# Five pairs of two experts run ahead of the last scatters, in a routed feed-forward kernel on one core

## The reference, cut to what matters

```python
xn = layernorm(x)                                  # 8192 tokens of 256
s = recurrent_attention(xn, W_in, W_g, W_out)      # a gated scan with 8 states, and projections
w, idx = gate(xn, wg)                              # 4 of 32 experts for every token
fe = idx.reshape(-1)
pos = (jnp.cumsum(one_hot(fe), axis=0) * one_hot(fe)).sum(-1) - 1
keep = pos < cap                                   # cap = 1280 rows for each expert, in token order
xe = xp[buf_tok].reshape(E, cap, DIM)
h = silu(xe @ w1) * (xe @ w3)                      # per expert, 256 x 256 weights
out = (h @ w2) * buf_w
y = zeros.at[buf_tok].add(out)
z = silu(xn @ sw1) * (xn @ sw3) @ sw2              # the shared expert
return x + s * silu(y + z)
```

## Time and profile before

| | |
|---|---|
| median of 3 runs | 1230.02 us (1228.3 to 1236.38) |
| the profiled execution | 1240.9 us, span 1239.0 us |
| phase A ends on TensorE | 482.2 us |
| the first expert matmul | 506.37 us |
| TensorE busy in the span | 82% |
| VectorE, POOL busy in the span | 66%, 61% |

### The profile page before, as it was taken

The page is one execution under the profiler, slowest core; times in us unless marked ns, Lnnn a source line. Parts: engine busy times, 40 slices in busy tenths (PEclk is TensorE's granted clock), DMA queues, the critical chain, the costliest instruction groups (busy, mean ns, idle before and its releaser), DMA issues.

```text
span 1239.0 us, 29972 instructions
## 1 busy us (share of the span) xinstructions
PE 1010.5 (82%) x7997; PEld 982.2 (79%) x7997; DVE 814.1 (66%) x2699; ACT 604.1 (49%) x1315; POOL 750.0 (61%) x600
## 2 busy tenths in 40 slices
PE   6767767778775763699999999999999999999900
PEld 5667666667664653699999999999999999999900
DVE  5656655555454454477777777777777777777659
ACT  5657656555664662244444444444444444445323
POOL 1255655566454656266776766667576767667785
PEclk7987988787887886799999999999999999999955
DMA  9123332223222334588787878878888889888579
GB/s 315 49 94 113 109 109 94 102 105 109 90 98 84 109 112 149 159 175 162 157 166 160 161 136 172 173 162 148 181 151 185 146 177 176 159 186 160 80 196 373
DMA packets 157611, 184.08 MB, mean 149 GB/s; under 512 B 19273, under 2 KB 147314, under 8 KB 157554
## 3 DMA queue, kind: packets, MB, share of 16 engines
q0 software_dynamic: 55936, 79.89, 33.6%
q1 hardware_dynamic: 100992, 103.50, 27.9%
q10 hardware_dynamic: 626, 0.01, 0.0%
HBM read 85.63 MB, written 101.35 MB: 151 GB/s over the span
## 4 chain that ended last, share of the span: by engine, by line
PE 62%; DVE 12%; another core or an unknown queue 9%; issue 8%; ACT 5%; DMA 2%; SPq 1%; POOL 1%; DVEq 0%; POOLq 0%; ACTq 0%
PE h L650 12%; PE h L652 12%; PE h L651 12%; PE yb L670 6%; PE yb L669 6%; PE yb L668 6%; PE xt L634 6%; DVE s_all L1399 2%; DVE s_all L1396 2%; DMA x_all<-L_attn_x 2%; DVE act L1127 1%; DVE raw L1140 1%; DVE raw L1149 1%; POOL y_sum L559 1%
## 5 line engine op out<-in xcount | busy, mean ns | idle before, releaser
L650 PE MATMUL h<-xh,w_hl 128*128 (+1 forms) x1392 | 419.6, 301 | 2.9 <-DVE xl L1121 2.5
L652 PE MATMUL h<-xl,w_hl 128*128 (+1 forms) x1392 | 405.0, 291 | 0.0
L651 PE MATMUL h<-xh,w_hl 128*128 (+1 forms) x1392 | 403.3, 290 | 0.8 <-issue 0.8
L543 POOL DMA_INDIRECT slot_rows<-rows,dest_idx x256 | 259.4, 1013 | 219.9 <-DVE dest_idx L1252 101.0
L559 POOL DMA_INDIRECT y_sum<-rows,y_idx x128 | 204.0, 1594 | 182.7 <-DMA y_sum<-yw,y_idx 80.3
L915 ACT ACTIVATE acth<-act 128x256 fp32r<-128x256 f32 x348 | 126.2, 410 | 328.9 <-PE yb L670 275.4
L650 PEld LDWEIGHTS h<-xh,w_hl 128*128 128x128 f32 x1392 | 275.0, 198 | 4.3 <-issue 3.1
L651 PEld LDWEIGHTS h<-xh,w_hl 128*128 128x128 f32 x1392 | 275.4, 198 | 2.0 <-issue 2.0
L652 PEld LDWEIGHTS h<-xl,w_hl 128*128 128x128 f32 x1392 | 275.2, 198 | 0.0
L1134 DVE TENSOR_TENSOR actl<-act,acth 128x256 fp32r<-128x256 f32 x348 | 132.4, 422 | 145.8 <-ACT acth L915 127.5
L668 PE MATMUL yb<-w_hl,acth 128*128 128x256 f32 x696 | 199.3, 286 | 9.2 <-DVE actl L1134 6.6
(11 more groups left out here) (217 smaller groups left out, 1532.4 us busy)
## 6 DMA issues: line engine op xcount, KB each, us to landing
rows<-slot_rows SPq DMA_DIRECT2D x143, 289.0 KB
raw<-L_ffn_w SPq DMA_DIRECT2D x96, 256.0 KB
slot_rows<-rows SPq DMA_DIRECT2D x32, 289.0 KB
x_all<-L_attn_x SPq DMA_DIRECT2D x16, 512.0 KB, 6.1
y_sum<-yw SPq DMA_DIRECT2D x32, 256.0 KB
out<-s_all SPq DMA_DIRECT2D x32, 256.0 KB, 6.1
slot_rows<-rows,dest_idx POOLq DMA_INDIRECT x256
w_hl<-y_sum POOLq DMA_DIRECT2D x12, 256.0 KB, 7.0
```

What stands on the lines that cost most here:

```text
L543: pool.indirect_dma_start(slot_rows, bass.IndirectOffsetOnAxis(dest_idx[slot][:, t, k:k + 1], 0), rows[slot][:, t, :], None, bounds_check= ...
L650: mm(out, high, xh[:, k, cols], start=(k == 0), stop=False)
L651: mm(out, low, xh[:, k, cols], start=False, stop=False)
L652: ins = mm(out, high, xl[:, k, cols], start=False, stop=(k == KD - 1))
```

## The change

The expert loop now covers experts 2 to 31. The pairs of experts 0 and 1 run ahead of it in an order written out by hand: (0,0), (0,1), (0,2), (1,0), (1,1), then (0,3), the fifth of 0 where there is one, (1,2), (1,3) and the fifth of 1. The first five do not wait for all scatters. VectorE keeps, after each group, how many rows experts 0 and 1 have so far (`seen_two`, 15 small additions); a second small matmul sums them, and six more steps turn them into `landed`: for each of the first three pairs of either expert, how far each `scattered` semaphore must have come. SP reads four of these values for each of the five early loads. The rows' buffers are laid out anew, the `y_out` buffers no longer lie in `rows[3]`, and POOL drains after (0,2), after (1,1) and after (0,3), where before it drained once for each expert.

```diff
+            def rows_landed(e, j):
+                first = (e * AHEAD + j) * SLOTS
+                return [sp.value_load(landed[0:1, first + n:first + n + 1], min_val=16 + SCATTERS * (n == 0),
+                                      max_val=ALL_SCATTERED) for n in range(SLOTS)]
+
-            def load_rows(e, j, buf, free=True, zeros_too=False):
+            def load_rows(e, j, buf, free=True, zeros_too=False, by_group=False, values=None):
...
+                if by_group:
+                    values = values or rows_landed(e, j)
+                    for n in range(SLOTS):
+                        sp.wait_ge(scattered[n], values[n])
...
-            sp.wait_ge(counts_ready, 1)
-            sp.wait_ge(zero_ready, 1)
-            store_zeros(0)
-            for n in range(SLOTS):
-                sp.wait_ge(scattered[n], 16 + SCATTERS * (GROUPS // SLOTS))
...
-            load_rows(0, 0, PAIRS - 1, False, zeros_too=True)
-            for n in range(3):
-                load_rows(0, n + 1, n, False)
+            sp.wait_ge(counts_ready, 1)
+            first_values = rows_landed(0, 0)
+            sp.wait_ge(counts_ready, 2)
+            sp.wait_ge(zero_ready, 1)
+            store_zeros(0)
+            sp.wait_ge(scattered[0], ALL_SCATTERED)
+            load_rows(0, 0, 3, False, zeros_too=True, by_group=True, values=first_values)
+            load_rows(0, 1, 0, False, by_group=True)
+            sp.wait_ge(scattered[1], ALL_SCATTERED)
+            load_rows(0, 2, 1, False, by_group=True)
             for n in range(3):
                 load_raw(1, n)
             store_zeros(1)
-            with sp.Fori(0, E - 2) as e:
+            sp.wait_ge(scattered[2], ALL_SCATTERED)
+            load_rows(1, 0, 2, False, zeros_too=True, by_group=True)
+            load_rows(1, 1, 3, by_group=True)
+            for n in range(3):
+                load_raw(2, n)
+            store_zeros(2)
+            for n in range(SLOTS):
+                sp.wait_ge(scattered[n], ALL_SCATTERED)
+            load_rows(0, 3, 0)
+            sp.wait_ge(counts_ready, 3)
+            fifth = is_fifth(0)
...
+            for body in first_three[1:] + next_two[:1]:
+                add_pair(body.y_buf)
+            pool.wait_ge(added[1], 32)
+            pool.wait_ge(added[2], 32)
+            pool.wait_ge(added[3], 64)
+            add_pair(next_two[1].y_buf)
+            add_pair(fourth_of_0.y_buf)
+            pool.wait_ge(added[PAIRS], fifth_adds(0))
+            pool.wait_ge(added[0], 48)
...
+            add_pair(third_of_1.y_buf)
+            pool.wait_ge(added[PAIRS], fifth_adds(count.fifths_now()))
+            pool.wait_ge(added[1], 64)
+            add_pair(fourth_of_1.y_buf)
...
+            splits_ready(0)
+            for body in first_three:
+                head_pair(body)
+            splits_ready(1)
+            for body in next_two:
+                head_pair(body)
+            head_pair(fourth_of_0)
...
+            pair((0, 1), 0, 64, True)
+            pair((2,), 0, 64)
...
+                if g < GROUPS - 1:
+                    v.tensor_tensor(seen_two[:, g + 1, :], seen_two[:, g, :], seen_new[:, 0:2], ALU.add)
                 v.tensor_tensor(seen[:, :], seen[:, :], seen_new[:, :], ALU.add).then_inc(seen_ready, 1)
```

More of the change, by code:

```diff
@@ L48 @@
 SCATTERS = 16 * GT * K
+ALL_SCATTERED = 16 + SCATTERS * (GROUPS // SLOTS)
+AHEAD = 3
 NORM_STEPS = 4
@@ L130, in build @@
             state_hl = sb_first("state_hl", [P, GN])
-        y_more = [sb(f"y_more{n}", [P, 2 * D]) for n in range(2)]
+            seen_two = sb_first("seen_two", [P, GROUPS, 2], BF16)
+        y_more = [sb(f"y_more{n}", [P, 2 * D]) for n in range(PAIRS)]
         meta = sb("meta", [P, 4, 2, 1 + E])
@@ L771, in _ @@
             pe.wait_ge(seen_ready, GROUPS + 1)
-            mm(cnt, ones[:, :], seen[:, :], start=True, stop=True).then_inc(cnt_ready, 1)
+            mm(cnt, ones[:, :], seen[:, :], start=True, stop=True)
+            mm(cnt_two, ones[:, :], seen_two[:, 1:GROUPS, :].rearrange("p g e -> p (g e)"),
+               start=True, stop=True).then_inc(cnt_ready, 1)
             count = PairCounter(pe, "pe")
@@ L786, in down_before, with pair @@
                 down(q + (A_PAIRS - 1), wts, [(y_ready, q * 2)])
+            pe.wait_ge(counts_ready, 3)
+            count.load_flags()
             look_ahead(0, PAIRS - 1, 1)
             pe.wait_ge(z_ready, 2 * A_PAIRS)
[L790 to L803, removed]
+            def pair(w_slot, next_buf, next_fill, w_before):
+                q = count.now()
+                up(q + A_PAIRS, w_hl[w_slot], bass.ds((q % 2) * PAIR, PAIR),
+                   lambda: look_ahead(q + 1, next_buf, next_fill))
+                if w_before is not None:
+                    down_before(q, w_hl[w_before])
@@ L981, in _, with pair, section @@
             count = PairCounter(sc, "act")
+            sc.wait_ge(counts_ready, 3)
+            count.load_flags()
             xhigh(A_PAIRS, region(0), (h3_ready, A_PAIRS - 1))
-            sc.wait_ge(counts_ready, 1)
-            count.load_flags()
-            def section(e, w_slot, is_first):
-                def body(slot):
[L988 to L992, removed]
+            def pair(splits=(), w_next=None, loads=None, after_down=False, slot=0):
+                q = count.now()
+                p = q + A_PAIRS
+                silu(p)
+                xhigh(p + 1, bass.ds(((q + 1) % 2) * PAIR, PAIR), (h3_ready, p))
+                act_high(p)
+                if after_down:
+                    sc.wait_ge(down_ready, p)
+                if splits:
+                    split_high(w_hl[w_next], loads, splits)
+                count.next(slot)
+            def section(e, w_slot):
+                def body(slot):
                     if slot < 3 and not (isinstance(e, int) and e == E - 1):
[L995 to L998, removed]
+                        pair((slot,), 1 - w_slot, e * 16 + 48, slot == 0, slot)
+                    else:
+                        pair(slot=slot)
                 slots(sc, count, body)
+            for n in range(3):
+                pair((n,), 1, 48, n == 0)
+            for _ in range(3):
+                pair()
+            with sc.If(count.next_flag() > 0):
+                pair(slot=PAIRS)
+            pair((0, 1), 0, 64, True)
+            pair((2,), 0, 64)
+            with sc.If(count.next_flag() > 0):
+                pair(slot=PAIRS)
             expert_loop(sc, section)
@@ L1364, in _, with pair @@
             v.memset(pad[:, 0:1], 0.0).then_inc(y_ready, 2)
+            ve.wait_ge(counts_ready, 3)
+            count.load_flags()
             take_meta(0, PAIRS - 1, 1)
             xlow(A_PAIRS, region(0), (h3_ready, A_PAIRS - 1))
-            ve.wait_ge(counts_ready, 1)
-            count.load_flags()
-            def section(e, w_slot, is_first):
+            def pair(next_buf, next_fill, before, splits=(), w_next=None, split=None, after_down=False, slot=0):
+                q = count.now()
+                p = q + A_PAIRS
+                take_meta(q + 1, next_buf, next_fill)
+                xlow(p + 1, bass.ds(((q + 1) % 2) * PAIR, PAIR), (h3_ready, p))
+                gate_act(p)
+                act_low(p)
+                if before is not None:
+                    take_y_before(q, *before)
+                if after_down:
+                    ve.wait_ge(down_ready, p)
+                if splits:
+                    split_low(w_hl[w_next], split, splits)
+                count.next(slot)
@@ L1371, in body, with head_pair, section @@
+            def head_pair(body, **more):
+                pair(body.next_buf, body.next_fill,
+                     None if body.prev_e is None else (body.prev_e, body.y_buf, body.y_uses), **more)
+            def section(e, w_slot):
                 def body(slot):
-                    q = count.now()
-                    p = q + A_PAIRS
                     fifths = count.fifths_now()
-                    take_meta(q + 1, slot, fifths + 1 if slot == PAIRS else next_fills(e, slot))
-                    xlow(p + 1, bass.ds(((q + 1) % 2) * PAIR, PAIR), (h3_ready, p))
@@ L1382, in body @@
                     if slot < 3 and not (isinstance(e, int) and e == E - 1):
[L1383 to L1386, removed]
+                        pair(*args, splits=(slot,), w_next=1 - w_slot, split=e * 3 + 7, after_down=slot == 0, slot=slot)
+                    else:
+                        pair(*args, slot=slot)
                 slots(ve, count, body)
+            for n in range(3):
+                head_pair(first_three[n], splits=(n,), w_next=1, split=7, after_down=n == 0)
@@ new lines, in _ @@
+            for body in next_two:
+                head_pair(body)
+            head_pair(fourth_of_0)
+            with ve.If(count.next_flag() > 0):
+                head_pair(fifth_of(0, count.fifths_now()), slot=PAIRS)
+            head_pair(third_of_1, splits=(0, 1), w_next=0, split=10, after_down=True)
```

(3 more changed lines are left out.)

108 lines of the change are left out of this document (80 added, 28 removed).

## The result

| | median | lowest to highest | runs |
|---|---|---|---|
| kernel before | 1233.20 us | 1228.30 to 1242.66 | 4 |
| changed kernel | 1346.34 us | 1345.39 to 1348.10 | 4 |

What follows compares the result with a forecast made beforehand. TensorE, busy 82% of the span, was taken as the bound, with POOL nearly as slow. Terms -5.0 + 2.6 + 0 + 0.7 = -1.7 us took 1240.9 to 1239.2, or 1228 as a median; range 1217 to 1242.

Steps and rivals of the forecast that it cites:

- small edits: VectorE's additions to `seen_two` and other little work around phase A: 0.7 us lost, between 0 and 1.5.
- SP's slow pace goes on: Rival: SP's new code stays slow, each gated load costs 9 us against a pair's 4.7; over 1242.3 us, chance 0.08.
- The advance of the first pair: Head, pair (0,0): starts sooner without waiting for all scatters; 5 us gained, between +9.3 and -1.
- the fourth rival: SP reaches its first load at 501 to 502, no pair starts sooner: 1234 to 1236 us, chance 0.12.
- the fast sum: SP's steps to the first `up` at expert-phase pace: 497.0 against 506.37, 9.3 us sooner.
- The pause inside the fifth pair: TensorE stands still because the rows of (0,3) load late: 2.6 us lost, between 0 and 4.8.
- The drains of POOL: Two more before pair (1,2), 8.6 us; expert 2's first add 9.7 us behind VectorE, covered by slack, no cost.
- the two splits of expert 2 in one body: Adds 0.7 us to VectorE's 3.5 of a pair's 4.7; priced at nothing.
- The value loads: SP's four register loads ahead of the first row load: about 0.5 us each, 2.0 in all.
- the head start is whole: Rival: advance near the limit set by the splits, 14.9 us, nothing late; under 1217.7 us, chance 0.08.

Runs made afterwards that it cites:

- the record: The first measurement of both kernels, nothing added: kernel before 1233.20 us, changed kernel 1346.34 us.
- after_pad24: The changed kernel with 24 idle semaphore increments on VectorE ahead of the expert loop: 1119.05 us, 0.988 of the kernel before.
- before_again: The kernel before, unedited, executed once more for a profile beside the later runs: 1132.44 us.
- after_split: `after_pad24` with expert 1's weights split one pair earlier: 1116.63 us, 0.985 of the kernel before.
- after_pad4: The changed kernel with 4 idle semaphore increments on VectorE ahead of the expert loop: 1227.56 us, against 1133.58 for the kernel before.

## Why the prediction was wrong

I predicted 1228 us, 1217 to 1242, and gave 0.08 to slower. It was 1346.

**The step that failed is one that was not taken.** The sum priced the head, the drains and small edits, and carried over the expert loop at 4.7 us a pair. That rests on the assumption that code that isn't edited keeps its speed when it is moved. The change adds some 400 VectorE instructions ahead of the loop, and the loop then lay over four blocks. There was a term missing; the runs showed it as 0 or as some 8 us for each of 13 turns, with no value between. It could not have been put there from the trace of before, where all that is to be seen is a q14 of 31 packets and no stall. It could have been a rival, since the section of the Trainium skill named above tells that a jump out of the window costs a fetch. By the table a loop of 268 lies badly in 11 of 128 places, so 0.09 would have been a fair chance for it; an estimate by the section's blocks of 256 is 11 of 256. Its price could not have been had from the trace of before.

**The rival "SP's slow pace goes on".** It ended on the right side, by luck, and its mechanism was wrong: SP was fast from 496.08 on, a gated load took less than a pair, and TensorE waited for rows once only, ahead of the first pair.

**The advance of the first pair: +5, between +9.3 and -1.** By the clock of the trace it was +0.7 in the record, the fourth rival. Counted from the end of phase A it was less: the first `up` came 28.2 us behind it (505.68 for 477.46), where it had come 24.1 behind (506.37 for 482.23), so the change made the head 4.1 us longer, below my lower bound of -1. TensorE's timeline of the changed kernel, with SP's below it:

```profile
477.27 0.19 PE L842 MATMUL pb<-seen_two,ones 128*128 128x30 bf16 x1
502.78 1.12 PE L703 MATMUL xt<-ident,rows 128*128 128x128 f32 x4 [25.32 <-DMA rows<-slot_rows]
505.68 0.57 PE L719 MATMUL h<-xh,w_hl 128*128 x1 [1.78 <-DVE xl L1229]
...
497.24 0.40 SPq L441 DMA_DIRECT2D slot_rows<-rows  x1
499.92 6.38 SPq L474 DMA_DIRECT2D rows<-slot_rows  x3
```

The first load left at 499.92, behind the four value loads of line 456, which at the slow pace fill 482.69 to 496.08; POOL's last scatter started at 492.79. So it was bound by SP, as predicted, and at the pace that I had given the smaller part of the weight: the four value loads alone took 13.4 us, where the fast sum has 2.0. Phase A ended 4.7 us sooner than in the kernel before (477.5 for 482.2, outside the 1.5 us that I allowed), and that was lost too.

In the later series SP was fast and the advance was 19.9 us, twice my upper bound. The fast sum isn't what was wrong by that much: phase A to first `up` is 18.0 us in `after_pad24`, and 497.0 less 482.2 is 14.8. What differs is the kernel before. The head start comes out of the time by which POOL's scatters lag behind phase A. In the record the last one starts 15.6 us behind phase A's end; in `before_again` phase A is shorter, POOL scatters with no pause over 0.31 us from 340 us on, and the last one starts at 388.60, 28.6 us behind. With the 24.1 us of the record, the 18.0 of `after_pad24` would give an advance of 6.1 by estimate, near the 5 that I took.

**The pause inside the fifth pair, 2.6 us for rows.** It was not there. There was one ahead of the fourth pair, for the third split of expert 1, 3.4 us in `after_pad24`. The change has `splits_ready(1)` directly behind the third pair: I had priced that split as what SP's weight load waits for, and not as what TensorE waits for. The size was near, the place and the cause wrong; `after_split` took it away. In the record TensorE stopped there as well, as the chain of waits shows:

```profile
523.14 0.69 DVE w_hl L1222
523.83 0.58 issue
524.41 0.38 PE h L719
```

**The drains of POOL.** Right. The timeline of POOL in `after_pad24`, and VectorE's first result of expert 2:

```profile
449.35 1.55 POOL L613 DMA_INDIRECT y_sum<-y_more,y_idx  x1 [4.50 <-DVE y_more L1479]
...
438.19 0.47 DVE L1479 TENSOR_SCALAR y_more<-yb,meta 128x256 f32<-128x256 f32 x1
```

POOL starts its first add of expert 2 10.7 us behind VectorE's result (predicted 9.7), TensorE goes on at 852 matmuls in 100 us through it, and VectorE never waits for a `y_out` buffer. "Nothing" was right for the two splits of expert 2 in one body as well, and the small edits cost nothing either (0.7 predicted): phase A ends at 359.73 in `after_pad24` and at 359.97 in `before_again`.

**The value loads** at 0.5 us each were about right: in `after_pad24` the TENSOR_LOADs of the early loads have a median of 378 ns (262 to 720, 20 of them), and the register instructions behind each take 0.17 us. The 600 ns that the prediction cites as a floor didn't show.

The sum of the head, with the code well placed and SP fast, is 19.9 - 3.4 - 1.6 = 14.9 us in spans (1130.6 to 1115.7), the last term being what is left. It is about what the clock took: from 398.7 to 402.1, behind the pause, TensorE's matmuls follow each other at 0.21 us and not at 0.12. My sum was a gain of 1.7, and the rival "the head start is whole" had 0.08. The 14.9 us are a gain over a kernel whose scatters lag by 28.6 us. At the level of the record the same sum with an advance of 6.1 leaves 1.1 us by estimate, and with SP's slow pace a loss: there the change had next to nothing to win, and the placement of the loop decided.

## What to carry to other kernels

A change that adds or removes instructions ahead of a long loop moves the loop, and here that was worth 7.7 to 8.3 us in each turn on an engine whose loop is some 270 instructions long. When a kernel is slower in a place that wasn't edited, look for "issue" at the jump back and for a higher packet count of the instruction queue, and put some idle instructions ahead of the loop before the change is thrown away. Try more than one number: 3 more changed nothing here, 9 and 23 were enough, and 22 made a fast kernel slow. In the later series 8% slower (`after_pad4`) became 1.2% faster, and 1.5% with the splits sooner. Before an advance is priced, see how far the work that it no longer waits for lags behind: here it was 16 us in one profile and 29 in another of the same kernel. Read what the consumer waits for at its own line (`splits_ready(1)`), not only what the producer's queue waits for.

## What the runs showed of the hardware

- VectorE's loop behaves as if its code was held in three blocks of 128 instructions. It was seen for a loop of 264 and one of 268, at nine places; the model is fitted to them, smaller blocks fit them too, and no run measured a block by itself.
- A loop over four blocks cost 7.7 to 8.3 us a turn and 4.6 or 4.7 more packets of 8 KB on q14 (60 more in 13 turns, 65 in 14, 70 in 15). Of 110 us in 13 turns, 77 were TensorE waiting and 34.5 TensorE's matmuls at a lower clock.
- The kernel before ran at 1233 us in the record and at 1133 to 1134 in three later series. In the first, SP's straight code behind phase A went in steps of 0.7 us and phase A was 122 us longer; in the others neither was so. The cause stays open: no experiment met the longer executions again. There the 113 us are put down to the placement by the same marks in the trace, not by a run with increments.
